# A shorter lead of the row maxima over the scores, and an earlier load for the second batch, in a four-layer kernel

## The chip, the cores and the metric

The kernel runs on one core of a Trainium2 chip. The metric is the device time of one execution in microseconds (us), as the median of several runs. The profile is of one execution of its own.

## What is computed

Four batches of 2048 tokens, 256 wide, go through four sublayers, each with a residual and a layer norm:

```python
x = L0_attn_x                                   # (4, 2048, 256)
x = _layernorm(x + _L0_attn_ref(x, ...))        # random-feature attention, exp(x @ orf.T)
x = _layernorm(x + _L0_ffn_ref(x, ...))         # gated net, inputs and weights in blockwise FP4
x = _layernorm(x + _L1_attn_ref(x, ...))        # softmax attention, the part that matters here
x = _layernorm(x + _L1_ffn_ref(x, ...))         # mixture of 8 experts, capacity 160

# _L1_attn_ref, 16 heads of 16, k and v through a latent of 64:
scores = jnp.einsum('bhqd,bhkd->bhqk', q, k) / np.float32(np.sqrt(HD))
attn = jax.nn.softmax(scores, axis=-1)
out = jnp.einsum('bhqk,bhkd->bhqd', attn, v)
```

## The kernel before

**A plan of units.** `make_plan` writes one list of small units of work, and five functions, one for each engine, walk this list and emit their own part of each unit in its order. So the order on every engine, and on SP, which issues nearly all DMAs, is the order of the list; engines meet only at semaphores. An engine that waits at one unit holds up all that stands behind it in its own queue.

**The softmax attention.** Work goes by groups n = 0 to 15: a group is four heads of one batch (b = n // 4). A group has four query blocks qc of 512 queries. Two streams run side by side:

- *Maxima.* Softmax subtracts each row's maximum. A unit `M` is two matmuls (`ps<-KM,QM`) into two PSUM banks, and `MR` is VectorE's reduction of them (`mx<-ps`, L1622). A query block has 32 such units. After its last one come `mx` (`mxr<-mx`, L1628), `R1` (TensorE transposes `mxr`, ScalarE copies it to `mres`) four units later, and `R2` eight units later: GpSimd splits `mres` into bf16 rows (L1936, L1938, L1940), and SP stores them with eight small DMAs `QS<-mrow` (L2109) as two more rows of the query operand.
- *Scores.* 64 steps for a group, 16 for a query block. A step is four score matmuls S (`ps<-QS,KS`, which wait for the stored maxima of their query block), four exponentials on ScalarE (`Pb<-ps`, L1368), and V, the product with the values of the step before (`ps<-Pb,VA`, L747). `ORDER` gives a step's order, `"SSMMSSVB"`: two of the maxima's units go into each step, and B is a unit of background work (preparing the next batch: `pt`, `pa`, `px`, `pp`, `ps`, `pv`; or finishing the last).

**What follows a query block.** When the last V of block (n, qc) is done, ScalarE copies the bank to `Ob` (`c1`). Then, in fixed steps of the next block (`OUT`): `oa` stores the denominators (`pk<-Ob`, SP), `ob` inverts them (`pk<-pk`, VectorE, step 6), `oc` writes them out (`rd<-pk`, SP, step 6), `od` reads them back spread over the heads (`den<-rd`, SP, step 8), `oe` multiplies (`den<-Ob,den`, GpSimd, L1869, step 11, which waits for that load), `og` stores the result (`aTb<-den`, SP). Steps are counted from the block's first.

**Loads of the maxima's operands.** While the maxima of a group's last query block run, `fm(n+1, i)` reloads `QM` and `KM` for head i of the next group, right behind that head's last maxima (four DMAs of SP, two `QM<-qd` and two `KM<-kd`, L2101). `fetch(n+1, i)` loads the score operands (`QS<-qd`, `KS<-kd`) at step 14 of each block.

**The passage before it.** The net ends with unit `dn` of token tile 63, its normalization `ap1`, and SP's store of the last rows to `x1d`. Eight units of maxima (`EARLY`) run among the last units of the net. `phase2` closes the net. Batch 1's rows are loaded to `xc2` (`pl(1, 0)`, `xc<-x1d`, L2080; it waits for the last `dn`, whose buffers it overwrites), and `pt(1, 0, k)` transposes them. Background units go in after every second unit of maxima until the first query block's maxima are stored; then, after `phase2b`, come `LEAD` more units of maxima, and the steps of scores begin.

Of the kernel before, what the change touches and what calls it, by code (L numbers as in the profile page):

```python
# [17 lines left out]
NT = 64  # L18
# [7 lines left out]
CAP = 160  # L26
ORDER = "SSMMSSVB"
START = 20
LEAD = 10

EARLY = 8
FETCH = 14
# [186 lines left out]
def make_plan():  # L219
    plan, prepared, ready, rows, bg = [], set(), set(), set(), []  # L220
# [3 lines left out]
    def background():  # L224
        while bg:
            units = next(bg[0], None)
            if units is None:
                bg.pop(0)
                continue
            plan.extend(units)  # L230
            prepared.update(u[1] for u in units if u[0] == "prepared")
            ready.update(u for u in units if u[0] == "ap2")
            return

    def maxima():
        pend, carry, age = [], [], 0
        for n in range(16):
            for qc in range(4):
                for i in range(4):
                    for q in range(4):  # L240
                        for h in range(2):
                            age += 1
                            if age in (4, 8) and pend:
                                carry.append(pend.pop(0))
                            yield carry + [("M", n, qc, i, q, h), ("MR", n, qc, i, q, h)]
                            carry = []
                    if qc == 3 and n < 15:
                        while groups[n + 1][0] not in prepared:
                            background()
                        carry.append(("fm", n + 1, i))  # L250
                carry += [("mx", n, qc)] + pend
                pend = [("R1", n, qc), ("R2", n, qc)]
                age = 0
        yield carry + pend

    mx = maxima()

    def maximum():
        units = next(mx, None)
        if units:  # L260
            plan.extend(units)
            rows.update(u[1:] for u in units if u[0] == "R2")
# [18 lines left out]
    def beside():  # L281
        units = next(side, None)
        if units:
            plan.extend(units)
            prepared.update(u[1] for u in units if u[0] == "prepared")
            if 0 in prepared:
                plan.extend(("fm", 0, i) for i in range(4))
# [3 lines left out]
    for T in range(-1, NT + 7):  # L291
        pair, last = T // 2 - 1, T - 4
        if T % 2 == 0:
            if 0 <= pair < NT // 2:
                plan.append(("qa", pair))
        elif 0 <= pair < NT // 2:
            plan.append(("qc", pair))
        if 0 <= last - 1 < NT:
            plan.append(("da", last - 1))
        if T % 4 == 3 and 0 < T < NT - 8:  # L300
            plan.append(("qx", T // 4 + 2))
        if T % 4 == 1 and T >= 9:
            plan.append(("st1", T - 9))
        if T % 4 == 2 and T >= 10 and T != NT + 2:
            plan.append(("ap1", T - 10))
        if T == 56:

            plan += [("ones", 0)] + [("fetch", 0, i) for i in range(4)]
        if (T + 1 < NT or 0 <= last < NT) and T != NT + 3:
            plan.append(("tt", T))  # L310
        for _ in range({NT + 1: 2, NT + 2: 3, NT + 3: 3}.get(T, 0)):
            maximum()
        if T == NT + 2:
            plan.append(("tt", NT + 3))
        if T == NT + 3:
            plan.append(("ap1", NT - 8))
        if T == NT:
            plan.append(("va0",))
        if T >= START:
            beside()  # L320
        if 0 <= T < NT:
            plan.append(("up", T))
        if T % 2 == 0 and 0 <= pair < NT // 2:
            plan += [("ha", pair), ("qb", pair)]
        if T % 4 == 3 and 0 < T < NT - 8:
            plan += [("xa", T // 4 + 2)] + [("xb", T // 4 + 2, i) for i in range(4)]
        if T in (6, 8, 10, 12):
            plan.append(("fold", T // 2 - 3))
        if 0 <= last < NT:
            plan.append(("dn", last))  # L330
        if T >= START:
            beside()
    while 0 not in prepared:
        beside()
    plan += [("pl", 1, 0), ("phase2",)]


    def output(part, n, qc):
# [10 lines left out]
    bg.append(prep_order(1))  # L349
    while (0, 0) not in rows:  # L350
        maximum()
        if len([u for u in plan if u[0] == "M"]) % 2 == 0 and ("mx", 0, 0) not in plan:
            background()
    plan.append(("phase2b",))
    for i in range(LEAD):
        maximum()
# [91 lines left out]

def program(nc, t, ctx):
    plan = make_plan()  # L450

    at, a_no, d_no = {}, {}, {}
# [1844 lines left out]
```

## Time and profile before

| | |
|---|---|
| median of 3 runs | 4779.27 us (4768.89 to 4782.6) |
| profiled execution | 4775.64 us, its span 4773.8 us |
| TensorE busy | 4480.3 us (94%) |
| VectorE busy | 3499.2 us (73%) |
| ScalarE busy | 2809.7 us (59%) |
| GpSimd busy | 1011.5 us (21%) |
| mean granted TensorE clock | 0.971 |
| maxima begin / first score / last maxima | 1446.7 / 1527.73 / 4456.1 us |

The attention's steps take some 2940 of the 4774 us. Busy time is that in which an engine executes; matmuls overlap, so TensorE's is no measure of distance from its peak. What is worth reading here are waits: a row's bracket tells how long the engine stood idle before the work and who ended that.

### The profile page before, as it was taken

Reading aid. Unit: us, or ns where it says so; the run is one execution under the profiler, and the core shown is the slowest. Engines: PE = TensorE matmul, PEld = TensorE weight load, DVE = VectorE, ACT = ScalarE, POOL = GpSimd, SP = SyncE. Lnnn points to the kernel's source line nnn. Section 1 sums busy time; section 2 is a strip of 40 time slices with the busy share of each in tenths; the row PEclk is TensorE's granted clock in tenths of the full one; section 3 lists DMA queues with packets and bytes.
Section 4 is the critical chain, followed back from the end, with each engine's and each line's share of the span. In section 5 each row is a group of like instructions: output and inputs, shape, how many; then the busy total and the mean of one; then the engine's idle time right before and its main releaser. Section 6 shows DMA issues by size and latency. Waiting matters only on the chain.

```text
span 4773.8 us, 65646 instructions
## 1 busy us (share of the span) xinstructions
PE 4480.3 (94%) x25500; PEld 1682.0 (35%) x25500; DVE 3499.2 (73%) x3850; ACT 2809.7 (59%) x5305; POOL 1011.5 (21%) x990
## 2 busy tenths in 40 slices
PE   8888888999997999999999999999999999999896
PEld 4444444666663222222222222222222232222285
DVE  2454446887887778888777888777888888888432
ACT  2222222333332778888777777777777757787721
POOL 2333334344521210000221110112111011100213
PEclk9999999999997999999999999999999999999998
DMA  3000100011212321211333222223222221222232
GB/s 102 24 24 21 60 10 19 9 49 61 75 73 67 126 90 66 65 42 69 117 93 111 66 74 77 78 102 120 73 80 74 64 70 45 86 68 80 73 113 54
DMA packets 230532, 330.69 MB, mean 69 GB/s; under 512 B 37031, under 2 KB 171753, under 8 KB 228169
## 3 DMA queue, kind: packets, MB, share of 16 engines
q1 hardware_dynamic: 227340, 318.63, 20.3%
q0 software_dynamic: 2880, 7.87, 0.8%
q8 instruction: 201, 3.29, 0.3%
q14 instruction: 111, 0.90, 0.1%
HBM read 218.95 MB, written 98.04 MB: 66 GB/s over the span
## 4 chain that ended last, share of the span: by engine, by line
PE 69%; DVE 10%; DMA 3%; POOL 3%; issue 2%; ACT 1%; SPq 1%; POOLq 0%; DVEq 0%; ACTq 0%
PE ps L747 67%; DVE mx L1622 4%; PE ps L750 2%; DMA pk<-Ob 1%; DVE stat L1446 1%; DVE hn L1440 1%; DMA x2d<-eb 0%; DVE hn L1601 0%; DMA rd<-pk 0%; DVE hn L1596 0%; DVE eb L1457 0%; DMA QS<-mrow 0%; ACT Pb L1368 0%; DVE hs L1432 0%; SPq L2109 0%
## 5 line engine op out<-in xcount | busy, mean ns | idle before, releaser
L1622 DVE TENSOR_REDUCE mx<-ps 128x1 f32<-128x1024 f32 x2048 | 2407.0, 1219 | 446.7 <-PE ps L747 443.4
L1368 ACT ACTIVATE Pb<-ps 128x512 f32<-128x512 f32 x4096 | 2202.6, 596 | 530.3 <-PE ps L747 526.7
L747 PE MATMUL ps<-QS,KS 98*128 98x512 bf16 x4096 | 1253.6, 387 | 15.9 <-ACT Pb L1368 7.4
L747 PE MATMUL ps<-Pb,VA 128*32 128x512 f32 x8192 | 1102.1, 610 | 0.1
L747 PE MATMUL ps<-KM,QM 64*128 64x512 bf16 x4096 | 660.5, 390 | 49.1 <-DVE mx L1622 47.3
L747 PEld LDWEIGHTS ps<-QS,KS 98*128 98x128 bf16 x4096 | 260.2, 98 | 1096.7 <-ACT Pb L1368 909.2
L747 PEld LDWEIGHTS ps<-KM,QM 64*128 64x128 bf16 x4096 | 179.5, 93 | 606.3 <-issue 354.5
L747 PEld LDWEIGHTS ps<-Pb,VA 128*32 128x32 f32 x8192 | 161.6, 108 | 401.7 <-issue 400.7
L1936 POOL CAST mrow<-mres 16x128 bf16<-16x128 f32 x64 | 18.0, 281 | 1292.4 <-ACT mres L1190 1292.4
L1494 DVE TENSOR_TENSOR phi<-ps,ns 128x1024 f32<-128x1024 f32 x64 | 78.3, 1223 | 219.4 <-PE ps L747 219.2
L747 PE MATMUL ps<-wdT,hT 128*128 128x256 f32 (+1 forms) x768 | 193.7, 395 | 15.5 <-DVE X L1607 14.1
L1215 ACT ACTIVATE phi<-phi 128x1024 f32<-128x1024 f32 x64 | 67.6, 1057 | 181.3 <-DVE phi L1494 181.3
L747 PE MATMUL ps<-wgT,xqT 128*128 128x352 f32 x512 | 168.7, 474 | 0.0
L1529 DVE RECIPROCAL rB<-ps 128x512 f32<-128x512 f32 x28 | 94.0, 3358 | 99.8 <-PE ps L747 99.8
L1869 POOL TENSOR_TENSOR den<-Ob,den 128x512 f32<-128x512 f32 x64 | 81.5, 1273 | 397.5 <-DMA den<-rd 397.4
L747 PEld LDWEIGHTS ps<-wdT,hT 128*128 128x128 f32 (+1 forms) x768 | 140.7, 192 | 68.3 <-issue 42.9
L747 PE MATMUL ps<-wuT,xqT 128*128 128x352 f32 x512 | 161.9, 459 | 0.0
L747 PE MATMUL ps<-qT,Wblk 128*128 128x512 f32 x256 | 132.9, 644 | 25.3 <-ACT phq L1276 25.3
L1862 POOL TENSOR_SCALAR vpe<-mv 128x4 f32<-128x4 f32 (+1 forms) x52 | 14.9, 287 | 617.8 <-DVE mv L1450 617.6
L1276 ACT ACTIVATE phq<-ps 128x1024 f32<-128x1024 f32 x56 | 57.4, 1024 | 138.1 <-PE ps L747 138.1
L747 PE MATMUL ps<-Wblk,kT 128*128 128x512 f32 x256 | 128.9, 628 | 9.7 <-DVE phi L1494 9.7
L1925 POOL CAST parts<-pres 128x1024 bf16<-128x1024 f32 x32 | 37.7, 1177 | 469.0 <-ACT pres L1190 443.6
(255 smaller groups left out, 4450.8 us busy)
## 6 DMA issues: line engine op xcount, KB each, us to landing
QM<-qd SPq DMA_DIRECT2D x128, 256.0 KB
KM<-kd SPq DMA_DIRECT2D x128, 256.0 KB
qd<-parts SPq DMA_DIRECT2D x96, 256.0 KB, 2.7
kd<-parts SPq DMA_DIRECT2D x96, 256.0 KB, 2.8
QS<-qd SPq DMA_DIRECT2D x64, 384.0 KB
KS<-kd SPq DMA_DIRECT2D x64, 384.0 KB
vdr<-vst SPq DMA_DIRECT2D x64, 256.0 KB, 2.5
den<-rd SPq DMA_DIRECT2D x64, 256.0 KB
```

The source lines that it names most:

```text
L747: return eng.matmul(out, a, b, start=start, stop=stop, skip_group_check=skip)
L750: return eng.transpose(out, a, ident[0:n, 0:n])
L1215: eng.activation(phi[n % 3], phi[n % 3], ACT.Exp, bias=0.0, scale=1.0).then_inc(act_phi, 1)
L1276: eng.activation(flat(way_of(C)["phq"][ht][:, 2 * g:2 * g + 2, :]), bank(b5, 2), ACT.Exp, bias=0.0, scale=1.0).then_inc(act_pq, 1)
L1368: eng.activation(Pb[(u - 1) % 9], o, ACT.Exp, bias=0.0, scale=0.25).then_inc(act_A, 1)
L1440: eng.tensor_tensor(blk(xn), blk(x), wide(rs, n // 16, 16), ALU.mult).then_inc(own, 1)
L1446: d = eng.bn_stats(stat[:, i % 4, j, :], x[:, j, :])
L1494: eng.tensor_tensor(phi[n % 3].rearrange("p (a b) -> p a b", a=16), bank(1, 2).rearrange("p (a b) -> p a b", a=16), wide(ns[C % 2][:, j, : ...
L1529: eng.reciprocal(f["rB"], bank(b7)).then_inc(dve_rec, 1)
L1622: eng.tensor_reduce(mx4[qc % 2][:, 4 * i + q, h:h + 1], o, AX, ALU.max).then_inc(dve_D, 1)
L1869: eng.tensor_tensor(den, Ob, den, ALU.mult).then_inc(pool_at, 1)
L1925: eng.tensor_copy(parts[:, 0, :, :], pres).then_inc(pool_ps, 1)
```

## The change

`pl(1, 0)`, the first load of batch 1's rows, moves from behind the last store of the net to ahead of it. The first background unit comes two units of maxima later (at made = 12, not 10), and `LEAD` goes from 10 to 7.

```diff
-LEAD = 10
+LEAD = 7
@@ the last passes over the net's tiles
         if T == NT + 3:
             plan.append(("ap1", NT - 8))
+        if T == NT + 4:
+            plan.append(("pl", 1, 0))
@@
-    plan += [("pl", 1, 0), ("phase2",)]
+    plan.append(("phase2",))
@@
     while (0, 0) not in rows:
         maximum()
-        if len([u for u in plan if u[0] == "M"]) % 2 == 0 and ("mx", 0, 0) not in plan:
+        made = len([u for u in plan if u[0] == "M"])
+        if made % 2 == 0 and made > EARLY + 2 and ("mx", 0, 0) not in plan:
             background()
```

The same units are in both lists, 11619 of them; the lines of the changed kernel are three further down. Before the first score the old list has 50 units of maxima and the new one 47, and this difference of three stays through all 16 groups. The last unit of maxima stands in step 998 before and in step 1000 after.

SP's queue at the end of the net, of before: two stores of rows to `x1d` (97, the blocks of tiles 56 and 60), then the load of batch 1.

```order
95 L2060 DMA x1d<-X 128x4x256 x2
96 L2073 DMA VA<-vdr 128x16x128
97 L2060 DMA x1d<-X 128x4x256 x2
98 L2080 DMA xc<-x1d 128x4x256
99 L2069 DMA KS<-in_ones 2x8192
100 L2080 DMA xc<-x1d 128x4x256
```

The same place of the change:

```order
95 L2063 DMA x1d<-X 128x4x256 x2
96 L2076 DMA VA<-vdr 128x16x128
97 L2063 DMA x1d<-X 128x4x256
98 L2083 DMA xc<-x1d 128x4x256
99 L2063 DMA x1d<-X 128x4x256
100 L2072 DMA KS<-in_ones 2x8192
101 L2083 DMA xc<-x1d 128x4x256
```

The load now stands between the two stores. On TensorE at the same place, of before (`wdT,hT` is the net's last `dn`, `identity,xc` the transposes of the loaded rows, two matmuls `KM,QM` a unit of maxima):

```order
1012 L747 MATMUL ps<-wdT,hT 128x256 x6
1013 L747 MATMUL ps<-KM,QM 128x512 x4
1014 L750 MATMUL ps<-identity,xc 128x128 x4
1015 L747 MATMUL ps<-KM,QM 128x512 x4
1016 L750 MATMUL ps<-identity,xc 128x128 x4
```

and of the change:

```order
1012 L750 MATMUL ps<-wdT,hT 128x256 x6
1013 L750 MATMUL ps<-KM,QM 128x512 x8
1014 L753 MATMUL ps<-identity,xc 128x128 x4
1015 L750 MATMUL ps<-KM,QM 128x512 x4
1016 L753 MATMUL ps<-identity,xc 128x128 x4
```

Four units of maxima stand ahead of the first transposes in place of two. On GpSimd, the first query blocks of the attention, of before: `mrow<-mres`, `mres<-mres,mrow`, `mrow<-mres` is an `R2`, `den<-Ob,den` an `oe`, and the four rows of `parts` and `pres` prepare batch 1.

```order
360 L1936 CAST mrow<-mres 16x128
361 L1938 TENSOR_TENSOR mres<-mres,mrow 16x128
362 L1940 CAST mrow<-mres 16x128
363 L1925 CAST parts<-pres 128x1024
364 L1927 TENSOR_TENSOR pres<-pres,parts 128x1024
365 L1929 CAST parts<-pres 128x1024
366 L1931 TENSOR_TENSOR parts<-pres,parts 128x1024
367 L1936 CAST mrow<-mres 16x128
368 L1938 TENSOR_TENSOR mres<-mres,mrow 16x128
369 L1940 CAST mrow<-mres 16x128
370 L1869 TENSOR_TENSOR den<-Ob,den 128x512
```

and of the change:

```order
356 L1939 CAST mrow<-mres 16x128
357 L1941 TENSOR_TENSOR mres<-mres,mrow 16x128
358 L1943 CAST mrow<-mres 16x128
363 L1928 CAST parts<-pres 128x1024
364 L1930 TENSOR_TENSOR pres<-pres,parts 128x1024
365 L1932 CAST parts<-pres 128x1024
366 L1934 TENSOR_TENSOR parts<-pres,parts 128x1024
367 L1872 TENSOR_TENSOR den<-Ob,den 128x512
368 L1939 CAST mrow<-mres 16x128
369 L1941 TENSOR_TENSOR mres<-mres,mrow 16x128
370 L1943 CAST mrow<-mres 16x128
```

The third `R2`, of block (0, 2), stood ahead of the first `oe`, of block (0, 0), and now stands behind it. That holds for every later pair `R2(n, qc)` and `oe` of two blocks before. Counted in the list, with steps numbered within a group, the units around the last query block of a group (its scores begin at step 48) stand so:

| unit | before, step | after, step |
|---|---|---|
| `fm(n+1, 2)` | 35 | 36 |
| `ob`, `oc` of block (n, 1) | 38 | 38 |
| `fm(n+1, 3)`, `mx(n, 3)` | 39, ahead of its M M | 40, between its M M |
| `od` of block (n, 1) | 40 | 40 |
| `R1(n, 3)` | 40, between its M M | 42, ahead of its M M |
| `oe` of block (n, 1) | 43 | 43 |
| `R2(n, 3)` | 42 | 44 |
| `og` of block (n, 1), `fetch(n+1, 2)` | 45 | 45 |

## Rows read from the trace of the kernel before

**Rows 1.** The page: the chain that ended last, share of the span by engine.

```profile
PE 69%; DVE 10%; DMA 3%; POOL 3%; issue 2%; ACT 1%; SPq 1%; POOLq 0%; DVEq 0%; ACTq 0%
```

**Rows 2.** The chain in order of time, 1440 to 1600 us: start, us, what.

```profile
1469.08 4.53 DMA xc<-x1d
...
1506.14 0.19 DVE mxr L1628
```

**Rows 3.** The timeline, 1461 to 1532 us: start, us, engine, work [idle before <-releaser].

```profile
1462.15 0.42 DVE L1607 TENSOR_TENSOR X<-ps,X 128x256 f32<-128x256 f32 x1 [1.21 <-PE ps L747]
1473.66 1.11 PE L750 MATMUL ps<-identity,xc 128*128 128x128 f32 x4 [10.41 <-DMA xc<-x1d]
1475.35 4.62 DVE L1622 TENSOR_REDUCE mx<-ps 128x1 f32<-128x1024 f32 x4 [8.68 <-PE ps L747]
1515.33 5.05 SPq L2109 DMA_DIRECT2D QS<-mrow  x8
1525.14 2.75 PE L747 MATMUL ps<-x2T,wkaT 128*128 128x512 f32 x4
1527.73 0.60 PE L747 MATMUL ps<-QS,KS 98*128 98x512 bf16 x2
```

**Rows 4.** Groups by line, 1880 to 2200 us: count, busy us, mean ns.

```profile
L747 PE MATMUL ps<-KM,QM 64*128 64x512 bf16 x484 | 75.7, 384 | 0.0
```

**Rows 5.** SP's timeline, 2918 to 2996 us, group 7.

```profile
2938.13 1.09 SPq L2101 DMA_DIRECT2D QM<-qd  x2
...
2947.59 0.52 SPq L2142 DMA_DIRECT2D den<-rd  x1
2948.15 5.49 SPq L2109 DMA_DIRECT2D QS<-mrow  x8
...
2984.46 0.57 SPq L2142 DMA_DIRECT2D den<-rd  x1
2987.60 4.95 SPq L2109 DMA_DIRECT2D QS<-mrow  x8
```

**Rows 6.** GpSimd's timeline, the same stretch.

```profile
2940.96 0.28 POOL L1936 CAST mrow<-mres 16x128 bf16<-16x128 f32 x1 [16.57 <-ACT mres L1190]
2960.85 1.26 POOL L1869 TENSOR_TENSOR den<-Ob,den 128x512 f32<-128x512 f32 x1 [18.76 <-DMA den<-rd]
2986.44 0.28 POOL L1936 CAST mrow<-mres 16x128 bf16<-16x128 f32 x1 [24.33 <-ACT mres L1190]
2989.53 1.27 POOL L1869 TENSOR_TENSOR den<-Ob,den 128x512 f32<-128x512 f32 x1 [1.96 <-DMA den<-rd]
```

**Rows 7.** TensorE's timeline at the start of group 7's last query block.

```profile
2962.26 0.60 PE L747 MATMUL ps<-QS,KS 98*128 98x512 bf16 x2 [1.69 <-DMA QS<-mrow]
```

**Rows 8.** Windows in group 7: busy by engine, granted clock, DMA share, GB/s.

```profile
2948.00:2958.00 10.00, 10.00 (x64) 2.25 (x64) 8.95 (x9) 8.50 (x16) 0.00 (x0) 1.00 0.26 105
2964.00:2967.00 3.00, 3.00 (x13) 0.41 (x14) 1.58 (x2) 1.90 (x5) 0.00 (x0) 0.50 0.25 54
```

**Rows 9.** GpSimd's `oe` and ScalarE's `Ob` copy in groups 1, 4, 14.

```profile
1863.11 1.27 POOL L1869 TENSOR_TENSOR den<-Ob,den 128x512 f32<-128x512 f32 x1 [16.18 <-DMA den<-rd]
1868.12 0.60 ACT L1190 ACTIVATE Ob<-ps 128x512 f32<-128x512 f32 x1 [0.16 <-PE ps L747]
2387.53 1.28 POOL L1869 TENSOR_TENSOR den<-Ob,den 128x512 f32<-128x512 f32 x1 [5.40 <-DMA den<-rd]
2399.90 0.60 ACT L1190 ACTIVATE Ob<-ps 128x512 f32<-128x512 f32 x1 [0.16 <-PE ps L747]
4296.39 1.27 POOL L1869 TENSOR_TENSOR den<-Ob,den 128x512 f32<-128x512 f32 x1 [15.35 <-DMA den<-rd]
4302.22 0.60 ACT L1190 ACTIVATE Ob<-ps 128x512 f32<-128x512 f32 x1 [0.16 <-PE ps L747]
```

**Rows 10.** DMA issues, us to landing; the longest waits, us, times, longest.

```profile
aTb<-den SPq DMA_DIRECT2D x256, 32.0 KB, 2.0
...
DVE pk L1637 <- DMA pk<-Ob: 31.0, 5, 11.5
```

## The prediction

> **What bounds the kernel now.** I first read the page's chain that ended last. TensorE holds 69% of it and VectorE 10% [rows 1]: the attention's steps run at TensorE's pace, so what TensorE stands idle there is lost whole, and what is taken out of a stretch in which VectorE sets the pace is won. Then the chain in order of time at the place of the change. The load of batch 1's rows is issued at 1469.08, behind the last store, and takes 4.53 us [rows 2]. The timeline shows what it costs: TensorE stands idle for 10.41 us until 1473.66 and VectorE 8.68 us until 1475.35, while the net had ended at 1462.15 [rows 3]. Last I read the timelines of SP, GpSimd and TensorE around a group's last query block, since the smaller lead acts in all 64 blocks. There lies the larger term.
>
> **The passage between net and attention.** The load now waits for the last `dn` alone (1462.15) and not for the normalization behind it, so it is issued some 6.5 us sooner and lands at about 1467.1. The two units of maxima put ahead of the transposes keep VectorE busy for 2 x 1.155 us (4.62 for four [rows 3]) until then, which closes its gap of 8.68 us; behind it the old pattern repeats. So I put the end of the first block's maxima at 1497.4 instead of 1506.14 [rows 2], with `R1`, `R2` and the stores of the rows as much sooner. These were issued from 1515.33 for 5.05 us [rows 3]; a small store took 2.0 us to land [rows 10], so the rows are there at 1520.4 + 2.0 - 8.7 = 1513.7. Three units fewer before the scores are 3.5 us of VectorE. TensorE no longer has the 2.75 us product of `x2T` (unit `pa`) just ahead of the first score; this and two transposes go into the steps. The first score then comes at about 1513.7 too, 14 us sooner than 1527.73 [rows 3]. Not all of it is kept: three units of maxima (75.7 / 484 x 2 = 0.31 us each [rows 4]), two transposes of 1.11 and that product of 2.75 [rows 3] must now be done where TensorE is the bound: 5.9 us at these durations, 3.4 if the last three run at the full clock and take half. I take 4.2: **-10 us**, bounds -8 to -11. The rest moves for nothing: `x1d`'s last store goes out behind the load, and is read only at the end; the background units run some ten steps later in batch 0, and are wanted only in group 3.
>
> **The smaller lead, in an ordinary block.** Three units fewer are one and a half steps, and since units come in pairs `mx`, `R1` and `R2` stand one, two and two steps later in the list. A step is 2.64 us: four of these matmuls go into one, and 484 of them into 320 us [rows 4]. The `Ob` copy of [rows 9] stands one step behind the first score of the next block. On the engines the maxima end 5.0 us later against the scores: two steps less one unit of TensorE. In a quiet block this is hidden. In block (8, 0) the rows of the maxima began on GpSimd at 2986.44, SP issued them from 2987.60 for 4.95 us [rows 5, 6], 2.0 more and they had landed at 2994.6; the block's scores began 16 steps behind 2962.26 [rows 7], at 3004.5, which leaves 10 us. Five of them are taken. On GpSimd `oe` is now ahead, and waits for `den<-rd`, which takes 5.1 us when nothing else is in flight (issued 2984.46, used 2989.53 [rows 5, 6]). That is over before the rows come. So 49 of the 64 blocks pay nothing.
>
> **The smaller lead, in the last block of a group.** Here the rows already come last. In group 7 TensorE stood idle for 1.69 us until 2962.26, and `QS<-mrow` ended it, though `mres` was ready at 2940.96 [rows 6, 7]. Between lie the loads `fm(8, i)`: SP begins the last at 2938.13, `den<-rd` at 2947.59 and the rows at 2948.15 [rows 5], and the DMA engines are at a share of 0.26 and 105 GB/s all through [rows 8]. So `den<-rd` takes not 5.1 but 13.3 us: `oe` starts at 2960.85 [rows 6]. The rows, issued behind it, land at 2962.2. Two things now happen.
>
> 1. The loads can only start when their head's last maxima are done, which is 5.0 us later. `fm(n+1, 0)` also stands behind `R2(n, 2)` on SP, which is as much later, and the four loads run back to back, so the last ends and `den<-rd` lands 5.0 us later: at 2965.8 in group 7's terms.
> 2. `R2(n, 3)` stands behind `oe` on GpSimd, where it stood ahead of it, and has to wait for `den<-rd`. Queued behind it are the three GpSimd instructions of `R2`, then SP's eight stores, then all of TensorE.
>
> The sum for group 7: `den<-rd` 2965.8, `oe` 1.3, the first cast to SP's first issue 1.2 (2986.44 to 2987.60), the first to the last issue 4.3 (7/8 of 4.95), landing 2.0, small gaps 0.2: the scores can start at 2974.8 instead of 2962.26, **12 us** later. In group 1: 1863.11 + 5.0 + 9.0 = 1877.1 against 1868.12 - 2.64 = 1865.5 [rows 9]: 11.6. In group 14, 4296.39 + 14.0 against 4302.22 - 2.64: 10.8. In group 4, where background work lengthens the steps and gives more time, 2387.53 + 14.0 against 2399.90 - 2.64: 4.3. I made this difference for all 15 groups that load for a next one, n = 0 to 14, in the same way, with each group's own step for the 5.0: eleven (n = 1 the first, 14 the last) give 9 to 12, in sum 113; the other four (0, 4, 8, 12) 2.5 to 7, in sum 20. Together **+133 us**. The bounds of each: at 5 us less (if the loads do not move) 133 - 15 x 5 = 58, and at 3 us more (below) 178.
>
> The Trainium skill says in "DMA: Bandwidth & Descriptors", section "Queues, rings and completion order", that each DMA engine takes descriptors in ring order, but that completion is not FIFO per issuing engine. By the second half a small `den<-rd` might land in its quiet 5.1 us, and group 7 would pay some 4 us, not 12. The trace speaks for the first half: 13.3 us in group 7.
>
> **The clock.** After the 1.69 us of idle time in group 7 the granted clock was 0.50 for 2964 to 2967, the lower level of 1.2 GHz, with TensorE fully busy [rows 8]. That costs 1.5 us. I add it to each of the 15 waits: **+22 us**; bounds 0 and 35.
>
> **The sum.** 4775.64 - 10 + 133 + 22 = 4920.6 for the profiled execution. The median of the runs shown lies 3.6 above it, so 4924 us, 3.0% above before.
>
> **The rivals.**
>
> - *The rows are late, but not held by `oe`* (4828 us). `den<-rd` lands early enough, and only the 5.0 us of the later maxima remain. The wait is then 5.0 less the room that the rows had. Group 7 had none (it waited), others 1 to 4 us by my reading, so 39 us of waits and 20 of clock, less 10. Against it: the 13.3 us of `den<-rd`. Chance 0.1. It is what the second half of the page's rule would make of the case.
> - *The rows come in time* (4769 us): not slower. Mechanism: the loads `fm` go out 5 us later, but also end sooner for lack of company, and `den<-rd` lands before its 5.1 us are over. The passage's 10 us are all that is left. It decides from the point at which `den<-rd` lands over 7 us before it does now; nothing in the rows shows such haste, and group 7 waits already. Within 0.3% of before. Chance 0.06, and 0.02 that the passage gives so much more that it is over 0.3% faster.
> - *VectorE is held too* (4970 us). `ob` on VectorE waits for `pk<-Ob`, which lies behind `fm(n+1, 1)` in the same queue; five such waits of 31.0 us stand in the trace [rows 10]. With the loads 5 us later it waits some 3 us in each of 15 groups, and maxima stop with it. I hold this to lie within the same wait of TensorE, since the chain through `den<-rd` still ends last. If it adds, 15 x 3 us. Chance 0.08.
>
> **Range and chances.** My forecast has 0.74, and its own range is 4870 to 4965 us. With part of the worse rival the range is 4845 to 4980. A difference of 0.3% (14 us) is about what a measurement of this kernel tells from none; slower by more: 0.92, within 0.06, faster 0.02.
>
> **What the changed profile would show.** In the passage TensorE's wait of 10.41 us for `xc<-x1d` shrinks to under 5 and the first score comes near 1514. In each of groups 0 to 14 TensorE waits 3 to 12 us for `QS<-mrow` once, at the last query block, and GpSimd's `mrow<-mres` there follows `den<-Ob,den` at once. The clock falls to 0.5 behind each. The other 49 blocks show no such wait. I am wrong if these waits are few or short: then the loads' place in the queue does not do what I read from groups 1 and 7; or if ordinary blocks wait as well: then 64 blocks pay, and the time is over 5000 us.

## The result and the profile after

The changed kernel takes 4991.39 us (median of 4 runs, 4976.78 to 5006.4) against 4774.08 for the kernel before beside it: 1.0465 times as long, 95% interval 1.0437 to 1.0492. The forecast was 4924 us with a range to 4980. The direction was right, and so was one of the two places where the time goes; the other was missed, and the size was too small. The profiled execution took 4996.52 us, its span grew from 4773.8 to 4994.6 by 220.8, and the mean granted clock fell from 0.971 to 0.953.

The page of the changed kernel: busy times and the chain (for the kernel before in [rows 1]).

```profile
PE 4538.4 (91%) x25497; PEld 1677.6 (34%) x25500; DVE 3505.7 (70%) x3850; ACT 2808.9 (56%) x5305; POOL 1008.8 (20%) x990
...
PE 52%; DMA 13%; DVE 10%; SPq 5%; POOL 4%; issue 2%; ACT 1%; POOLq 0%; DVEq 0%; ACTq 0%; another core or an unknown queue 0%
```

TensorE held 69% of the chain and holds 52%; DMAs went from 3% to 13%, SP's queue from 1% to 5%. The units of work are the same, but they are now waited for. Its waits, changed kernel (us, times, longest):

```profile
POOL den L1872 <- DMA den<-rd: 1889.5, 63, 59.1
...
PE ps L750 <- DMA QS<-mrow: 102.1, 15, 10.8
...
PE ps L750 <- DVE mx L1625: 80.3, 86, 7.2
...
DVE pk L1640 <- DMA pk<-Ob: 61.2, 12, 11.5
...
PE ps L750 <- DMA KS<-kd: 49.7, 11, 9.9
```

The same rows of the kernel before:

```profile
POOL den L1869 <- DMA den<-rd: 397.4, 61, 38.5
...
PE ps L747 <- DVE mx L1622: 54.2, 76, 4.0
...
PE ps L747 <- DMA KS<-kd: 4.9, 1, 4.9
PE ps L747 <- DMA aTb<-den: 4.0, 1, 4.0
...
PE ps L747 <- DMA QS<-mrow: 3.4, 2, 1.7
```

That is the account of the span: `QS<-mrow` +98.7, `KS<-kd` +44.8, VectorE's maxima +26.1, `xc<-x1d` -10.4 (no such wait is left), `aTb<-den` -4.0, together +155.2; and TensorE's own busy time +58.1, for the same matmuls at a lower clock (a score matmul took 393 ns in the mean, 387 before). Sum 213.3 of 220.8 us; the other 7.5 us I have not placed.

**The passage.** Timeline of the changed kernel, to be read beside [rows 3]:

```profile
1464.24 0.36 SPq L2083 DMA_DIRECT2D xc<-x1d  x1
...
1469.35 1.12 PE L753 MATMUL ps<-identity,xc 128*128 128x128 f32 x4
...
1478.15 2.36 DVE L1625 TENSOR_REDUCE mx<-ps 128x1 f32<-128x1024 f32 x2 [2.47 <-PE ps L750]
...
1516.61 1.01 PE L750 MATMUL ps<-QS,KS 98*128 98x512 bf16 x2 [1.45 <-DMA QS<-mrow]
```

The load goes out at 1464.24 in place of 1469.08, the transposes begin at 1469.35 with no idle time ahead, VectorE's longest gap there is 2.47 us in place of 8.68, and the first score comes 11.1 us sooner.

**The last block of group 1.** GpSimd, SP and TensorE of the changed kernel:

```profile
1868.62 1.26 POOL L1872 TENSOR_TENSOR den<-Ob,den 128x512 f32<-128x512 f32 x1 [57.58 <-DMA den<-rd]
1869.83 0.28 POOL L1939 CAST mrow<-mres 16x128 bf16<-16x128 f32 x1
```
```profile
1855.95 0.51 SPq L2145 DMA_DIRECT2D den<-rd  x1
...
1870.97 4.96 SPq L2112 DMA_DIRECT2D QS<-mrow  x8
...
1907.87 4.96 SPq L2112 DMA_DIRECT2D QS<-mrow  x8
...
1916.21 0.76 SPq L2124 DMA_DIRECT2D KS<-kd  x1
```
```profile
1877.02 1.03 PE L750 MATMUL ps<-QS,KS 98*128 98x512 bf16 x2 [6.46 <-DMA QS<-mrow]
...
1923.98 0.60 PE L750 MATMUL ps<-QS,KS 98*128 98x512 bf16 x2 [2.92 <-DMA KS<-kd]
```

`oe` waits for `den<-rd`, the first cast of `R2` follows it without a gap, SP's stores begin 1.1 us later, and TensorE resumes at 1877.02 after 6.46 us. The forecast's 1877.1 is the same number by luck: it was on the time base of the kernel before and meant a score 11.6 us late. The second wait was not in the forecast: the operands of group 2, issued at 1916.21 behind the stores of 1907.87, are not there when its scores are due.

### The profile page after: what moved, and what is told of

Same layout as the page of the kernel before. It is cut to its first block, busy times and chain, and to the rows that moved or that the text cites. A ratio compares the mean times of both kernels' runs of the same rounds, so it can differ in the third digit from the quotient of the medians.

```text
span 4994.6 us, 65643 instructions
## 1 busy us (share of the span) xinstructions
PE 4538.4 (91%) x25497; PEld 1677.6 (34%) x25500; DVE 3505.7 (70%) x3850; ACT 2808.9 (56%) x5305; POOL 1008.8 (20%) x990
## 4 chain that ended last, share of the span: by engine, by line
PE 52%; DMA 13%; DVE 10%; SPq 5%; POOL 4%; issue 2%; ACT 1%; POOLq 0%; DVEq 0%; ACTq 0%; another core or an unknown queue 0%
PE ps L750 51%; DVE mx L1625 5%; DMA den<-rd 4%; DMA pk<-Ob 3%; DMA rd<-pk 3%; SPq L2112 2%; DMA KS<-kd 2%; SPq L2104 1%; PE ps L753 1%; SPq L2089 1%; POOL pres L1930 1%; DVE stat L1449 1%; POOL parts L1934 1%; SPq L2154 1%; DVE hn L1443 1%
## 5 line engine op out<-in xcount | busy, mean ns | idle before, releaser
L750 PE MATMUL ps<-QS,KS 98*128 98x512 bf16 x4096 | 1283.6, 393 | 158.5 <-DMA QS<-mrow 102.1
L750 PE MATMUL ps<-Pb,VA 128*32 128x512 f32 x8192 | 1119.5, 619 | 0.1
L750 PE MATMUL ps<-KM,QM 64*128 64x512 bf16 x4096 | 674.5, 396 | 77.5 <-DVE mx L1625 73.8
L750 PE MATMUL ps<-wdT,hT 128*128 128x256 f32 (+1 forms) x768 | 193.6, 395 | 15.6 <-DVE X L1610 14.1
L1583 DVE TENSOR_TENSOR hh<-ps,sg 128x704 f32<-128x704 f32 x64 | 56.5, 883 | 93.4 <-PE ps L750 89.2
```

The costliest lines, as they stand in the source:

```text
L750: return eng.matmul(out, a, b, start=start, stop=stop, skip_group_check=skip)
L1583: eng.tensor_tensor(hh[p % 2][:, 704 * b:704 * b + 704].rearrange("p (a b) -> p a b", a=2), bank(2, 2).rearrange("p (a b) -> p a b", a=2)[ ...
```

## The experiments

Waits are those of TensorE in the attention unless another engine is named. The ratio is to the kernel before timed beside it, with its 95% interval. That kernel's median lay between 4765.39 and 4778.28 us in the three sessions, so ratios are to be compared, not medians.

**The lead alone, both ways.** The change with its old lead:

```diff
-LEAD = 7
+LEAD = 10
```

> The changed kernel with LEAD = 10 again: the early load and the later first background unit alone. Theory 1 (all of the loss comes from the smaller lead, and the passage gives back what its two gaps were): 4764 us, 10 us under the kernel before, ratio 0.998; the wait of 10.41 us for the rows of batch 1 is under 1 us, the first score some 9 us earlier than before, and the attention shows the same few waits for the stored maxima as before (3.4 us in sum). Rival (the early load takes the queue from something else): 4774 or more, with a new wait in the passage.

Measured: 4770.76 us, 0.9992 (0.9981 to 1.0003). `xc<-x1d` is waited for no longer, `QS<-mrow` 3.7 us. And the kernel before with the new lead alone:

```diff
-LEAD = 10
+LEAD = 7
```

> The kernel before with LEAD = 7 and nothing else. Theory 1: the whole loss and a little more, 4991 + 10 = 5000 us, ratio 1.047, with 15 waits of TensorE for the stored maxima of some 100 us in sum and some ten for the next group's score operands of some 45. Rival (the other two parts of the change carry part of the loss): clearly under 4991.

Measured: 5002.65 us, 1.0478 (1.0462 to 1.0493). Its waits:

```profile
PE ps L747 <- DMA QS<-mrow: 98.4, 14, 10.0
...
PE ps L747 <- DMA KS<-kd: 49.5, 12, 9.7
```

The whole loss is the lead's. The passage's edit gives 4 us by the first kernel and 6 by the second (1.0478 less 1.0465), neither clear of the intervals.

**One maximum more.** The change with `LEAD = 8`. The maxima stand almost as late, but `R2(n, qc)` is ahead of `oe` again, in the same step 43.

> The changed kernel with LEAD = 8: one unit of maxima more. The maxima and their loads stand only one unit earlier than with 7, but R1 and R2 stand one step earlier and with this R2 is ahead of the multiplication oe on GpSimd. Theory 1 (it is the order of R2 and oe that costs, and R2's stores ahead of the next fetch): most of the loss is gone, waits of 1 to 5 us in 15 blocks, 40 us in sum, hardly a wait for score operands, 4820 us, ratio 1.01. Theory 2 (it is the loads of the next group's maxima that come too late, in any order): the loss falls by about one unit of three and a half, to 4940 us, ratio 1.035.

Measured: 4778.62 us, 1.0001 (0.999 to 1.0012). Both expectations missed: less is lost than either said.

```profile
PE ps L750 <- DMA KS<-kd: 12.1, 8, 4.8
...
PE ps L750 <- DMA QS<-mrow: 4.4, 8, 1.0
```

Two of the three units taken away cost nothing that can be told; the third costs over 4%. It makes `R1` and `R2` one step later still, and it changes the order of `R2` and `oe` (and of one pair more, shown below).

**The order alone.** The kernel before, lead 10, with `oe` ahead of `R2`:

```diff
-OUT = {0: ("oa",), 5: ("ob", "oc"), 7: ("od",), 10: ("oe",), 12: ("og",)}
+OUT = {0: ("oa",), 5: ("ob", "oc"), 7: ("od",), 8: ("oe",), 12: ("og",)}
```

> The kernel before with its lead of 10, and oe moved from step 11 to step 9 of a block, ahead of R2 on GpSimd: only the order of the two is made as in the changed kernel, the maxima and their loads keep their time. Theory 1: each last block of a group waits for den<-rd without the 5 us of the later loads, 15 waits of 1 to 7 us, 60 us in sum, and R2's stores stand late ahead of the fetch also in quiet blocks, which costs some 30 us for score operands: 4880 us, ratio 1.022. Theory 2 (lateness of the loads alone): no change, 4775 us.

Measured: 4950.26 us, 1.0386 (1.0369 to 1.0404), with the maxima as early as ever. The mechanism is the expected one, its cost more (1.022 was expected). Its waits, and GpSimd in group 1:

```profile
PE ps L747 <- DMA QS<-mrow: 85.3, 12, 10.0
...
PE ps L747 <- DMA KS<-kd: 32.1, 10, 7.5
```
```profile
1880.45 1.26 POOL L1869 TENSOR_TENSOR den<-Ob,den 128x512 f32<-128x512 f32 x1 [56.94 <-DMA den<-rd]
1881.66 0.28 POOL L1936 CAST mrow<-mres 16x128 bf16<-16x128 f32 x1
```

The order alone is enough for a loss four fifths as large. It also makes waits for `KS<-kd`: the rows' stores are late at the first block of a group as well, and the fetch stands behind them on SP.

**The order taken out of the change.** Lead 7, with `oe` behind `R2`:

```diff
-OUT = {0: ("oa",), 5: ("ob", "oc"), 7: ("od",), 10: ("oe",), 12: ("og",)}
+OUT = {0: ("oa",), 5: ("ob", "oc"), 7: ("od",), 12: ("oe", "og")}
```

> The changed kernel with the lead of 7 kept, and the multiplication oe moved from step 11 to step 13 of a block, so that R2 stands ahead of it on GpSimd; the loads and everything else stay where they are. Theory 1: the stored maxima no longer wait for den<-rd, waits of 4 to 6 us in place of 6 to 11 in the last blocks, 50 us in sum; the fetch for the next group still stands behind R2's stores, so those waits of 45 us in sum stay: 4910 us, ratio 1.03. Theory 2 (the loads' lateness alone): as the changed kernel, 4990 us, ratio 1.045.

Measured: 4915.1 us, 1.0289 (1.0273 to 1.0305). Waits and GpSimd in group 2:

```profile
PE ps L750 <- DMA KS<-kd: 54.2, 12, 9.8
...
PE ps L750 <- DMA QS<-mrow: 27.0, 9, 5.5
```
```profile
2036.40 0.28 POOL L1939 CAST mrow<-mres 16x128 bf16<-16x128 f32 x1 [46.10 <-ACT mres L1193]
...
2047.60 1.28 POOL L1872 TENSOR_TENSOR den<-Ob,den 128x512 f32<-128x512 f32 x1 [10.07 <-DMA den<-rd]
```

The rows no longer wait for `den<-rd`, and three quarters of the waits for `QS<-mrow` go. Those for `KS<-kd` stay: the maxima's lateness makes them too. It does so in steps. In group 2 SP begins the rows' stores, with the fetch behind them, 18.4 us ahead of the time at which the first score is due in the kernel before, 15.8 us with `LEAD = 8` and 13.2 with 7, in the changed kernel and in this one; the waits are none, 0.66 and, with 7, 2.92 and 4.89 us.

Two of this version's waits for `KS<-kd`, in groups 7 and 11, are 9.83 and 9.71 us long (9.92 and 9.81 in the changed kernel), and they come from another order that the third unit changes. GpSimd in the changed kernel, group 7:

```profile
2909.51 0.23 POOL L1865 TENSOR_SCALAR vpe<-mv 128x4 f32<-128x4 f32 x1 [9.27 <-DVE mv L1453]
...
2910.82 0.28 POOL L1939 CAST mrow<-mres 16x128 bf16<-16x128 f32 x1
```

`vpe<-mv` belongs to a background unit, the layer norm's statistics of a finished batch, in step 59 of the group before. `R2(n, 0)` is in step 60 with `LEAD = 7` and behind it; with 8 it is in step 59 and ahead of it, and groups 7 and 11 have no wait. No run moved this pair alone. So there are two kinds of cause, the orders and the lateness, each of which makes operands late, and their costs do not add: `oe` ahead of `R2` alone costs 3.9%, the lateness with the `vpe` order 2.9%, all together 4.65%.

**The fetch of the operands, alone and with the order.** The change with `FETCH = 12` in place of 14 (two steps sooner, ahead of the rows' stores on SP):

> The changed kernel with FETCH = 12 in place of 14: the score operands of the next group are asked for at the end of step 13 of a block (of GpSimd's and TensorE's units nothing moves), so SP issues them ahead of R2's eight stores. Theory 1 (the waits for KS<-kd are SP's doing, which has R2's late stores and the four stores of og ahead of the fetch): those waits of 49.7 us in 11 places go to under 10, the waits for the stored maxima stay at 100 us or grow a little, since the rows now land behind a load: 4935 us, ratio 1.034. Rival (the operands are late because the DMA engines are full): the waits for KS<-kd stay near 50 and the time near 4990.

Measured: 4935.61 us, 1.0367 (1.0341 to 1.0392). No wait for `KS<-kd` is left, as expected, and those for `QS<-mrow` grow to 139.3 us. The same with `oe` behind `R2`:

> The changed kernel with the lead of 7 and both moves: oe behind R2 on GpSimd, and the fetch ahead of R2 on SP. Theory 1: what is left of the loss is the loads of the maxima's operands that come 5 us late, and VectorE's waits for pk<-Ob: 4850 us, ratio 1.016. Rival (the two waits are one, and hide each other): no better than the better of the two alone, over 4905.

Measured: 4912.24 us, 1.0305 (1.0285 to 1.0324), no better than the order alone. That is the rival; theory 1 missed. Of the 23 waits for `QS<-mrow`, 116.9 us, 14 with 76.7 us stand at last blocks, where the fetch now goes ahead of the rows' stores, and eight with 38.7 us in the middle of a group, where the changed kernel has none. Block (1, 1) is one of these eight, and SP and TensorE show what happens there:

```profile
1764.57 0.71 SPq L2124 DMA_DIRECT2D KS<-kd  x1
1765.82 0.76 SPq L2126 DMA_DIRECT2D VA<-vdr  x1
1766.63 11.78 SPq L2112 DMA_DIRECT2D QS<-mrow  x8
```
```profile
1779.50 1.03 PE L750 MATMUL ps<-QS,KS 98*128 98x512 bf16 x2 [8.79 <-DMA QS<-mrow]
```

`VA<-vdr` is a third load, which only the first fetch for a group has. Directly behind it the eight small stores took 11.78 us to issue, and 11.8 to 12.7 in five such blocks; in most of the others they took 4.96, at 1599.89 right behind `KS<-kd` too. So the waits for `KS<-kd` (54.2 us) went and those for `QS<-mrow` grew by more (from 27.0), while VectorE's maxima were waited for less (57.0 us, from 79.3).

**VectorE's part.** In the change, with `oe` behind `R2` as before, `ob` and `oc` go two steps later and `od` one, so that VectorE does not stop for `pk<-Ob`. The line, beside that of the change:

```diff
-OUT = {0: ("oa",), 5: ("ob", "oc"), 7: ("od",), 10: ("oe",), 12: ("og",)}
+OUT = {0: ("oa",), 7: ("ob", "oc"), 8: ("od",), 12: ("oe", "og")}
```

> The changed kernel with its lead of 7 and oe behind R2 (as in e4_oe_behind), and VectorE's inversion ob with its store two steps later. Theory 1 (VectorE stands at ob for pk<-Ob, which the late loads hold up, 59 us in 12 places, and TensorE's waits for maxima, 79 us where 54 were before, come from it): TensorE's waits for VectorE go back to about 55, those for score operands stay or grow, since og is later: 4895 us, ratio 1.025 (e4 had 1.029). Rival (the waits for VectorE are a consequence of the other waits): no change, ratio 1.029.

Measured: 4969.32 us, 1.0399 (1.0369 to 1.043), 54 us more than without these shifts; both expectations missed. VectorE's wait went from 59.2 to 29.5 us as meant, and TensorE's for the maxima from 79.3 to 54.9, but `QS<-mrow` is back at 98.4. SP in group 2:

```profile
2032.76 2.35 SPq L2139 DMA_DIRECT2D rd<-pk  x1
2048.39 0.53 SPq L2145 DMA_DIRECT2D den<-rd  x1
2048.97 4.96 SPq L2112 DMA_DIRECT2D QS<-mrow  x8
```

`rd<-pk` now goes out behind the last loads, where it stood ahead of them. `den<-rd` has to wait for it on SP (15.6 us from one issue to the other), and the rows, ready on GpSimd at 2034, stand behind `den<-rd`. The hold has moved from GpSimd's queue to SP's.

**More lead.** The change with `LEAD = 12`, 14 and 18, and the kernel before with 12.

> The changed kernel with LEAD = 12: the early load with a longer lead. If the lead only buys time, this removes the last waits for stored maxima and for KS<-kd (3.4 and 4.9 us in the kernel before) and VectorE's for pk<-Ob, and pays two units of maxima more ahead of the scores: 4765 to 4772 us, ratio 0.999, the same within what is measured. Rival (a longer lead shifts the loads fm into the quiet chain of den<-rd and pk<-Ob of the block before): slower, 4780 or more.

> The kernel before with LEAD = 12 and nothing else. Theory 1 (the passage's early load gives some 10 us in any case, and the longer lead the rest of what the version with LEAD = 12 and the early load has won): 4765 to 4775 us beside a before of 4770, ratio 0.999. Rival (the two gaps of the passage are covered by the longer lead, so that the early load adds nothing to it): as good as with the early load, ratio 0.997.

> The changed kernel with LEAD = 14. Theory 1 (the lead only has to hold R2 ahead of oe and of the fetch, more of it buys nothing, and each unit ahead of the scores costs 1.2 us of VectorE's time less the 0.3 us of TensorE that it takes out of the steps): as with 12 or 2 us more, ratio 0.997. Rival (the rows still land late in the last blocks, and each unit more takes from that): 5 us less than with 12, ratio 0.996.

> The changed kernel with LEAD = 18, where the loads of the next group's maxima come five and a half steps earlier than with 7. Theory 1: 3 to 6 us more than with 14, since nothing waits for the rows any more and only the passage grows. Rival: the loads fm now run into fetch and pk<-Ob of the block before and new waits come up; 10 us more or over.

| kernel | median us | ratio | `QS<-mrow` | `KS<-kd` | maxima | VectorE for `pk<-Ob` |
|---|---|---|---|---|---|---|
| change, 12 | 4751.42 | 0.9969 (0.9959 to 0.9979) | 8.9 | 5.5 | 52.4 | 28.9 |
| before, 12 | 4781.24 | 1.0004 (0.9991 to 1.0017) | 8.3 | 13.4 | 48.6 | 27.2 |
| change, 14 | 4840.92 | 1.0132 (1.0103 to 1.0161) | none | 18.4 | 103.7 | 87.7 |
| change, 18 | 4772.14 | 0.9987 (0.9972 to 1.0002) | none | 6.3 | 66.1 | 44.6 |

The passage's edit with lead 12 is the one version whose interval lies wholly below the kernel before, by 0.3%; it was expected level with it. Lead 14 was a surprise: 1.0132 where 0.997 was expected, and 18 came 1.4% below it where a few us more were expected. The kernel before with 12 is level with itself at 10, so the early load is worth its part there. SP and VectorE of that kernel in group 7:

```profile
2958.95 0.56 SPq L2133 DMA_DIRECT2D pk<-Ob  x1
...
2973.26 0.34 SPq L2139 DMA_DIRECT2D rd<-pk  x1
2973.65 4.95 SPq L2112 DMA_DIRECT2D QS<-mrow  x8
```
```profile
2972.98 0.25 DVE L1640 RECIPROCAL pk<-pk 128x16 f32<-128x16 f32 x1 [11.90 <-DMA pk<-Ob]
```

With 14, the list has `fm(n+1, 2)` ahead of `oa(n, 1)` and `fm(n+1, 3)` ahead of `ob` (steps 33 and 37, against 33 and 38). `pk<-Ob` goes out behind three heads' loads, 14 us pass until VectorE has it, and the maxima stop with it. With 12 only `fm(n+1, 3)` has passed `ob`. The rows' stores have passed `od` as well (`R2(n, 3)` in step 40), as the lines of SP show. With 18 both orders of `fm` hold as with 14, but the loads are two more steps earlier, and further pairs have swapped: `R2(n, 3)` is ahead of `ob`, and `fm(n+1, 0)` ahead of `od` of block (n, 0). Which of these relieves `pk<-Ob` is not shown; none was tried by itself.

## Why the prediction was right and wrong

**The passage: -10 us.** The mechanism is right. TensorE's wait is gone, and the first score came at 1516.61 (forecast 1513.7). The net ended 2.1 us later in this profiled execution, at 1464.24, which is not the edit's doing: with `LEAD = 8` and the same passage it ended at 1462.03. Counted from the net's end the first score is 13.2 us sooner, where the forecast had 14. What is kept of it is less sure. Three pairs that differ in this edit alone, with leads 10, 7 and 12, differ by 0.1, 0.1 and 0.35%: 4, 6 and 17 us, two below the bounds of 8 to 11 and one above, the last from two sessions.

**The hold of `R2(n, 3)` behind `oe`: +133 us.** The mechanism is shown: at lead 8, where `oe` is behind again, the loss is gone, and at lead 10 the order alone costs 3.9%. In the trace, the waits for `QS<-mrow` at last blocks are 100.7 us (102.1 less the first score's 1.45), in 14 of the 15 groups. The four groups with background work have 19.7 us of them (forecast 20), the other eleven 80.9, where the forecast had 113. Part of what is missing stands under another name. In group 7, for which I had 12 us, VectorE and TensorE of the changed kernel:

```profile
3050.22 0.25 DVE L1640 RECIPROCAL pk<-pk 128x16 f32<-128x16 f32 x1 [8.37 <-DMA pk<-Ob]
```
```profile
3051.60 0.61 PE L750 MATMUL ps<-KM,QM 64*128 64x512 bf16 x2 [7.24 <-DVE mx L1625]
...
3081.25 1.04 PE L750 MATMUL ps<-QS,KS 98*128 98x512 bf16 x2 [5.48 <-DMA QS<-mrow]
```

VectorE stopped first, and TensorE paid 7.24 there and 5.48 at the rows, 12.7 together. Group 11 is alike (7.15 and 6.44). Over the kernel 100.7 and the whole 26.1 of the maxima make 127, which is the most that this term can be. Groups 1 to 3 have 5.3 to 6.5 us of `QS<-mrow` and no wait for the maxima over 2.2, so there the 9 to 12 of the forecast were too much. Of the rival "VectorE is held too" the first half came true (`pk<-Ob` waited for 12 times, 61.2 us, was 5 and 31.0). In groups 7 and 11 its price was not added but lay within the same delay, as the forecast held; no run takes it out by itself.

**"So 49 of the 64 blocks pay nothing."** This step failed, the first of the two: the forecast put the ordinary blocks at nothing, and they cost 44.8 us. For block (8, 0) I asked whether the rows land in time, and they do. I did not ask what stands behind them on SP: four `aTb<-den`, then the fetch of the next group's operands, at step 61, one step behind `R2(n+1, 0)`, now at 60. If the maxima are 5.0 us later, so is the fetch behind their stores. The kernel before, SP and the first score of group 2:

```profile
1889.17 4.96 SPq L2109 DMA_DIRECT2D QS<-mrow  x8
...
1897.51 0.75 SPq L2121 DMA_DIRECT2D KS<-kd  x1
```
```profile
1907.56 0.60 PE L747 MATMUL ps<-QS,KS 98*128 98x512 bf16 x2
```

In the changed kernel the load was waited for until 1923.98, 7.0 us after its issue ended at 1916.97. In the kernel before that gives 1898.26 + 7.0 = 1905.3, 2.3 us ahead of the score. The fetch moved by 18.7 us (1897.51 to 1916.21), the score's due time by 13.5 (1907.56 to 1921.06): 5.2 us of lateness less 2.3 of room is the 2.92 measured. The kernel before could have told all of it: its one wait for `KS<-kd` ended at 3983.47, 7.0 us after that issue's end, too (group 13, where `vpe<-mv` stands ahead of `R2` already). The waits grew by 44.8 us, to 49.7 in eleven groups, and 19.7 of these stand in groups 7 and 11, where `vpe<-mv` had come ahead of `R2` on GpSimd, as shown above. The forecast's own sign of error, ordinary blocks that wait as well, is what came; it had no chance of its own.

**The clock: +22 us.** The second miss: 58.1 measured, above my bound of 35. TensorE in the changed kernel behind the wait in group 6, and windows there, to be read beside [rows 8]:

```profile
2868.81 1.04 PE L750 MATMUL ps<-QS,KS 98*128 98x512 bf16 x2 [10.77 <-DMA QS<-mrow]
```
```profile
2869.00:2872.00 3.00, 3.00 (x12) 0.46 (x14) 1.57 (x2) 1.69 (x4) 0.00 (x0) 0.50 0.27 55
2872.00:2875.00 3.00, 3.00 (x16) 0.44 (x8) 1.20 (x2) 1.76 (x4) 0.00 (x0) 0.72 0.36 119
```

The granted clock was 0.50 (1.2 GHz) from 2868.81 to about 2873.7, 4.9 us at half the pace, which costs 2.4 us and not the 1.5 that I took from behind a wait of 1.69. And there are not 15 such waits but 26, with eleven for `KS<-kd`. The slow stretches behind all 26 are 3.4 to 6.7 us long, 4.8 in the mean; as an estimate 26 x 2.4 = 62 us. The kernel before has three such waits, with 11.1 us of slow stretches.

With the measured terms in place of the forecast's, 4775.6 - 14 (the waits for `xc<-x1d` and `aTb<-den`) + 127 + 45 + 58 = 4992, against 4996.5. That is the account of the first section once more and proves nothing by itself; it shows which terms were short: 45 us at nothing, and 36 of the clock.

**The rivals that fell.** "Not held by `oe`" and "in time" need `den<-rd` early. In the changed kernel it took 12.7 us in group 1, from 1855.95 to 1868.62. The Trainium skill's "DMA: Bandwidth & Descriptors", section "Queues, rings and completion order", has each DMA engine take descriptors in ring order, with completion not FIFO per issuing engine. The trace fits the first half. For the second it is no test: `den<-rd` is not small, as the prediction has it, but moves 256 KB, as much as each `QM<-qd` and `KM<-kd` ahead of it, and a small load that overtakes large ones is shown by no run here.

## What to carry to other kernels

Where every engine walks one list, a lead measured in units is also a set of orders between chains. Before changing it, write down for each in-order queue, SP's as well, which waiting instruction passes which; here the two settings 8 and 7 differ by 4.6%, most of it from a pair that swapped (3.9% by that pair alone), and 12 and 14 by 1.6%, where the swaps are read from the list and not tried one by one. And when work is made later, follow it past the load that you look at to all that stands behind it in its queue, and ask each for its own room.

## What was not expected of the hardware

Eight small stores took 4.96 us to issue on SP in most blocks and 11.8 to 12.7 directly behind `VA<-vdr`, in five blocks of the version with both moves. The DMA engines' share was 0.80 in the first 6 us of the one shown, and 0.37 in the quick case at 1599.89; that the share is the reason is not shown. So the order of short and long transfers also sets when SP is free for the next.

The price of a stall in clock does not follow its length. In the changed kernel a wait of 10.77 us left TensorE at the lower level for 4.9 us, one of 10.84 for 3.8, and one of 2.99 for 6.0; this is behind the last two:

```profile
3699.36:3703.36 4.00, 4.00 (x16) 0.59 (x16) 2.35 (x2) 2.17 (x4) 0.00 (x0) 0.53 0.25 46
4379.77:4385.77 6.00, 6.00 (x20) 0.85 (x22) 2.36 (x2) 3.27 (x7) 0.00 (x0) 0.50 0.00 0
```

In the kernel with `LEAD = 8` fourteen waits for operands of 0.20 to 1.07 us were followed by no stretch at the lower level at all (the changed kernel has one of 0.39 us with 6.7 us behind it). This fits that its many short waits cost nothing that can be told, and that a few us more of lateness cost so much.
